# Layer 0's experts on token rows sorted by expert in DRAM, in tiles of 256 rows, instead of all experts on all tokens

## The reference

```python
x = _layernorm(x + _L0_attn_ref(x, ...))   # a linear recurrence over the sequence, then an MLP
x = _layernorm(x + _L0_ffn_ref(x, ...))    # top 2 of 8 experts
x = _layernorm(x + _L1_attn_ref(x, ...))   # attention, 16 heads of 8
x = _layernorm(x + _L1_ffn_ref(x, ...))    # top 2 of 4 experts, each expert an attention
```

```python
probs = softmax(input @ Wg)                       # 8 experts
top_vals, top_idx = top_k(probs, 2)               # shares: top_vals / their sum
xm = input[None] * moveaxis(mask, -1, 0)[..., None]
h = relu(einsum('ebsd,edh->ebsh', xm, W1) + b1)   # 128 -> 256
y = einsum('ebsh,ehd->ebsd', h, W2) + b2          # 256 -> 128
out = sum(y * moveaxis(scores, -1, 0)[..., None], axis=0)
```

## Time and profile before

| | us |
|---|---|
| median of 3 runs | 1557.26 (1551.56 to 1564.39) |
| the profiled execution, in all | 1544.68 |
| its span | 1542.9 |
| mean granted clock of TensorE, share of full | 0.911 |

### The profile page before, as it was taken

The page is one execution under the profiler, slowest core; times in us unless marked ns, Lnnn a source line. Parts: engine busy times, 40 slices in busy tenths (PEclk is TensorE's granted clock), DMA queues, the critical chain, the costliest instruction groups (busy, mean ns, idle before and its releaser), DMA issues.

```text
span 1542.9 us, 31463 instructions
## 1 busy us (share of the span) xinstructions
PE 1311.5 (85%) x12320; PEld 786.5 (51%) x12320; DVE 1017.0 (66%) x2422; ACT 767.9 (50%) x1260; POOL 525.6 (34%) x863
## 2 busy tenths in 40 slices
PE   4899999999655879889888899998989989988884
PEld 1566666667422335455445555555545545554543
DVE  3677667775444667777687777777777767757520
ACT  3334444433132356566465665665655656653540
POOL 1000010100342235346354454453544542442421
PEclk7999999999755879899899999999999999999986
DMA  7000000000000000101101011011010110110111
GB/s 206 1 1 1 1 1 1 0 1 1 0 1 9 9 2 9 38 11 33 31 13 42 18 26 37 8 42 31 13 42 5 39 36 9 42 36 10 32 34 36
DMA packets 34730, 35.03 MB, mean 23 GB/s; under 512 B 20070, under 2 KB 28440, under 8 KB 32536
## 3 DMA queue, kind: packets, MB, share of 16 engines
q1 hardware_dynamic: 34584, 33.03, 9.1%
HBM read 28.93 MB, written 2.88 MB: 21 GB/s over the span
## 4 chain that ended last, share of the span: by engine, by line
PE 44%; DVE 28%; SPq 7%; ACT 7%; POOL 5%; issue 5%; DMA 3%; DVEq 0%; ACTq 0%; POOLq 0%
PE ps L1367 17%; PE ps L634 14%; DVE mneg_e L1191 7%; PE ps L1445 7%; SPq L832 3%; PE ps L1468 3%; SPq L828 2%; DVE mneg_l L1191 2%; DVE acc L596 2%; DMA sums_l<-o_l 1%; SPq L850 1%; ACT probs L1038 1%; POOL q_low L915 1%; DMA sums_e<-o_e 1%; DVE equal L1217 1%
## 5 line engine op out<-in xcount | busy, mean ns | idle before, releaser
L1038 ACT ACTIVATE probs<-ps 128x1024 f32<-128x1024 f32 x384 | 389.8, 1024 | 244.9 <-PE ps L1367 243.9
L1191 DVE TENSOR_REDUCE mneg_e<-ps 128x2 f32<-128x512 f32 x512 | 337.1, 685 | 64.3 <-PE ps L1367 61.4
L1367 PE MATMUL ps<-k_high,q_high 32*128 32x256 f16 x1024 | 160.5, 283 | 50.6 <-DVE mneg_e L1191 41.3
L1191 DVE TENSOR_REDUCE mneg_l<-ps 128x2 f32<-128x512 f32 x256 | 167.8, 682 | 53.9 <-PE ps L1367 52.3
L1367 PE MATMUL ps<-q_high,k_high 32*128 32x256 f16 x1024 | 141.3, 276 | 4.1 <-ACT probs L1038 3.5
L1445 PE MATMUL ps<-probs,v_e 128*32 128x256 f32 x2048 | 138.6, 389 | 6.7 <-ACT v_e L1063 4.6
L1367 PE MATMUL ps<-q_low,k_high 32*128 32x256 f16 x1024 | 140.4, 273 | 0.0
L1367 PE MATMUL ps<-q_high,k_low 32*128 32x256 f16 x1024 | 139.6, 271 | 0.0
L428 ACT ACTIVATE h_moe<-ps,b 128x512 f32<-128x512 f32 x128 | 81.0, 684 | 116.9 <-PE ps L634 116.9
L634 PEld LDWEIGHTS ps<-w,h_moe 128*128 128x128 f32 x1024 | 122.1, 192 | 16.9 <-issue 16.7
L634 PE MATMUL ps<-w,h_moe 128*128 128x128 f32 x1024 | 124.6, 275 | 0.0
(11 more groups left out here) (216 smaller groups left out, 2393.6 us busy)
## 6 DMA issues: line engine op xcount, KB each, us to landing
on_e<-scratch_e SPq DMA_DIRECT2D x64, 256.0 KB, 4.6
on_l<-scratch_l SPq DMA_DIRECT2D x128, 32.0 KB, 1.9
sums_l<-o_l SPq DMA_DIRECT2D x128, 2.0 KB, 1.7
q_high<-shiftT_e SPq DMA_DIRECT2D x128, 2.0 KB
sums_e<-o_e SPq DMA_DIRECT2D x128, 4.0 KB, 1.7
out<-y SPq DMA_DIRECT2D x16, 128.0 KB, 2.0
w<-in_w SPq DMA_DIRECT2D x1, 1024.0 KB
qT<-shiftT_l SPq DMA_DIRECT2D x64, 2.0 KB
```

Source lines behind the costliest of these rows:

```text
L1038: act.activation(probs[:, probs_slot(r, i)].rearrange("p j s -> p (j s)"), s_banks(i).rearrange("p j s -> p (j s)"), ACT.Exp, scale=0.5 if ...
L1191: v.tensor_reduce(to, tiles(max_bank(k)), axis=AX, op=ALU.max, negate=True).then_inc(kind.max_used, 1)
L1367: return pe.matmul(o, l, r, start=start, stop=stop)
```

## The change

1. **Steps.** The 16 steps per chunk stay as the distance of two chunks, but each job gets a step of its own in a table `AT`, from -46 (`x_squares`) to 4 (the last scatters). A job with step s of chunk k is written at step s + 16 k. All of layer 0 up to the router is written this way, without expert products.
2. **Routing.** After the two experts are chosen, TensorE multiplies the 0/1 choice with a triangular and an all-ones matrix (`ranks`), which gives each token's rank among those of its expert. VectorE makes row numbers of it (`places`). GpSimd writes each tile of 128 tokens twice to DRAM, each row to its place (8 indirect DMAs per chunk). DRAM has one region for each expert, for each of two groups of 4 chunks; the regions are zeroed beforehand from SBUF (12 DMAs, 18.9 MB).
3. **Units.** When a group is complete, a table of tiles (256 rows of one expert each) is computed. A unit is two tiles; a group has 12 units (24 tiles, enough for any distribution). Per unit SyncE reads the table, loads two tiles of tokens (2 x 128 KB) and two experts' weights (2 x 329 KB) and stores two tiles of outputs over the tokens; TensorE transposes, multiplies to hidden and back; ScalarE copies and applies relu; VectorE adds b2.
4. **Sums.** GpSimd gathers each token's two outputs (8 indirect DMAs per chunk); VectorE adds them, times the shares, to x and normalizes.
5. **Order.** All layer 0 steps; the 12 units of group 0; the 12 units of group 1, between them the sums of group 0 (three pieces after each unit) and periods -6 to -4; then the periods from -3 on, with a piece of group 1's sums after every second slot.
6. **Smaller.** The gate is tanh, with its half in `wo0`, so there is no reciprocal; `mixer_scale` and `mlp_scale` are multiplied into weights once; GpSimd adds x and x1 (`xx`); scoreT and the b2 product are gone.

```diff
+STEPS = 16
+AT = {
+    "x_squares": -46, "x_rstd": -45, "xn": -43, "xT": -42, "xT_copy": -41, "kv_mm": -40, "k_copy": -39, "r_mm": -39,
...
+    "ranks": -4, "places": -3, "scatter": (-2, -1, 2, 4),
+}
...
-            for c in range(-2, CHUNKS + 1):
-                for i in range(STEPS if c < CHUNKS else LAST_STEPS):
-                    yield True, c, i
...
+            for u in range(FIRST_STEP, LAST_STEP + 1):
+                yield "layer0", u, None
+            for n in range(-1, UNITS + 1):
+                yield "experts", 0, n
+            prepared = [("attention", r, i) for r in range(FIRST_PERIOD, EARLY_PERIODS) for i in range(SLOTS)]
+            summed = list(sums_of(0))
+            done = 0
+            for n in range(-1, UNITS + 1):
+                yield "experts", 1, n
+                yield from summed[3 * (n + 1):3 * (n + 2)]
+                upto = len(prepared) * max(n, 0) // UNITS
+                yield from prepared[done:upto]
+                done = upto
...
+                    for t in range(CT):
+                        for k in due(u, AT["scatter"][t]):
...
+                            for n in range(2):
+                                pool.indirect_dma_start(by_expert[g], bass.IndirectOffsetOnAxis(ap=places[:, n, at:at + 1], axis=0),
+                                                        x_all[:, at, :], None).then_inc(z.scattered[g], DMA)
...
+                        if m == 0 and t == 0:
+                            for n in range(2):
+                                pool.wait_ge(ex.stored[n], DMA * PAIR * (UNITS // 2) * (g + 1))
...
+                    if 0 <= n < UNITS:
+                        q = UNITS * g + n
+                        act.wait_ge(ex.hidden_ps, q + 1)
...
+                                last = act.activation(h_moe[:, q % 2, k, at], hidden_bank[:, k, at], ACT.Relu, bias=b1)
...
+                        if t == 0:
+                            v.wait_ge(ex.gathered[k % 2], DMA * 2 * CT * (k // 2 + 1))
+                        token = k * CT + t
+                        for n in range(2):
+                            add = v.scalar_tensor_tensor(x_all[:, token, :], gathered[:, k % 2, n, t, :], shares[:, n, token:token + 1],
+                                                         x_all[:, token, :], ALU.mult, ALU.add)
+                            link(add)
```

## The result

The changed kernel takes 1569.46 us in the median of 11 runs (1559.95 to 1576.85); the kernel before, in turns with it, 1553.71 us (11 runs). The ratio is 1.0095 with a 95% interval of 1.0056 to 1.0133: slightly slower, at the very edge of the 1% bound. The forecast was 1581 us; the span forecast was 1566.8, the span of the profiled execution is 1565.2.

The account below looks back on a forecast made before the run. Layer 0 was taken as bound by TensorE, 224 of its 404 us being expert products. Forecast span: 437.5 to period -3, plus 24, plus 1105.3, 1566.8 us; 1581 us after scaling to the median; range 1500 to 1655.

Parts of the forecast that it names:

- The price p: GpSimd's time to issue one indirect DMA of 128 rows, for 64 scatters and 64 gathers; taken as 1.2 us.
- Rival 1: Faster through cheap issue: 0.43 us per indirect DMA, as on SyncE; 1518 us of span, 1532 as median; chance 0.32.
- rival 3: Slower through dear issue: VectorE's short SBUF operations delay scatters and gathers; at p = 2, 1658 us; chance 0.17.
- Rival 2: No change: p near 0.9, or the clock stays at 1.00 through the dense steps; about 1556 us; chance 0.18.
- Dense steps: Layer 0 ahead of the units: bound by hand-overs, 28.5 us per full chunk, ending at 247.5 us.
- 2 "of some 5" for the clock: Dense steps: half clock lengthens the cycle by some 5 us, 2 of them counted; pitch 28.5 instead of 26.5 us.
- Group 0's units: First twelve units: 5.6 us each, waiting for relu; 72 us in all, to 319.5.
- Rival 4: SyncE bounds the units: a table load near 1.5 us makes a unit 6.8 us; 29 more, 1610; chance 0.08.
- Group 1's units: Second twelve units: 34 us for the first two, 27 for the next four, 54 for the rest; sum 115 us.
- the remaining seven carry two prepared periods: End of group 1's units: 39 + 25 = 64 us one after the other, taken as 54, partly hidden in waits.
- The tail: From v_e's fill to the end: group 1's sums add 19 us in period -3 and 5 in period -2.
- All 224 us saved are spent: Layer 0's saved expert products go into longer dense steps and 187 us of units; v_e's fill stays near 437 us.

Follow-up runs that it names:

- e7: Changed kernel with GpSimd's sum xx 3 steps later (-26 in place of -29); 1563.71 us, ratio 1.0076 to the kernel before.
- e3: Changed kernel with the sums of group 0 begun two units later in group 1; 1580.18 us, ratio 1.0170 to the kernel before.

## Why the prediction was right, and where it was not

**The price p.** The choice of 1.2 us was the decisive one and right: 0.95 us busy, 1.26 from issue to issue. It was taken from another operation, a four-column power, and no run shows that the two have to do with each other: in that the number is luck. Rival 1 (0.43) and rival 3 (2 us) fall with it; rival 3's "from p about 1.1 it alone puts the time over 1% slower" was wrong, as p was 1.26 and the time 0.95% longer. Rival 2 had no change from p near 0.9 or from the clock staying at 1.00; the clock did not stay, and the issue's distance, which counts, is 1.26. By the Trainium skill (SBUF — State Buffer, "SBUF: two separate sides") a DMA issued by GpSimd that takes 0.62 us alone took 3.1 us beside a VectorE operation that holds the shared ports. Here the 64 scatters took 0.95 to 1.23 us to issue and 2.2 us in the median, 4.3 at most, from issue to landing beside VectorE's work, so the trace shows neither figure.

**Dense steps: 13 us short.** 247.5 was forecast for their end, the first scatter of the last chunk is at 260.7. The first chunk's is at 66.4 (64 forecast), and the pitch is 30.4, 30.4, 30.4, 30.7, 28.3 where the sum had 28.5. Step by step: x3 possible 7.7 us after the scatters' start, measured 7.7 (127.12 to 134.86, when x_all starts); the x root done at 11.4, measured 11.6; xn done at 12.3, measured 13.5. Here xn's price was wrong, 1.88 us for 0.87, because xx on GpSimd starts at the same moment. From xn to the next scatter 14.2 at full clock, and 2 "of some 5" for the clock, 16.2: measured 16.9. In e7, with the short xn and the clock at 0.83, xn to the next scatter took 13.6 us (109.68 to 123.29) and the whole pitch 26.2, the full-clock forecast being 26.5. So the chain was right and the two terms that failed are xn beside xx (1.0) and the clock (2.7 us over the forecast's 14.2, 3.3 over e7's 13.6, and not 2). The expectation that TensorE would be under 60% busy failed as well: 69%, since at the lower clock its work is longer.

**Group 0's units: right.** 72 us forecast, 69.7 measured (260 to 330), 5.5 us apart. TensorE in order of time, changed kernel:

```profile
282.70 0.63 PE L916 MATMUL ps<-ident,tokens 128*128 128x128 f32 x4 [1.42 <-DMA tokens<-by_expert]
...
288.60 2.02 PE L926 MATMUL ps<-expert_w,h_moe 128*128 128x128 f32 x16 [1.31 <-ACT h_moe L623]
...
294.10 2.02 PE L926 MATMUL ps<-expert_w,h_moe 128*128 128x128 f32 x16 [1.31 <-ACT h_moe L623]
```

They wait for relu, as forecast, and twice for tokens (1.42 and 1.53 us). Rival 4 (SyncE) did not occur.

**Group 1's units: 16 us too long.** VectorE in order of time:

```profile
346.42 1.51 DVE L813 SCALAR_TENSOR_TENSOR x_all<-gathered,shares,x_all 128x128 f32<-128x128 f32 x4 [16.31 <-DMA gathered<-by_expert,places]
348.24 0.75 DVE L788 TENSOR_TENSOR y_tokens<-ps,expert_w 128x256 f32<-128x256 f32 x2 [0.30 <-PE ps L926]
...
362.15 0.17 DVE L1613 TENSOR_TENSOR k_w<-qk_w 128x8 f32<-128x8 f32 x1 [4.92 <-POOL v_l L1217]
...
363.10 0.73 DVE L788 TENSOR_TENSOR y_tokens<-ps,expert_w 128x256 f32<-128x256 f32 x2
...
428.77 0.76 DVE L788 TENSOR_TENSOR y_tokens<-ps,expert_w 128x256 f32<-128x256 f32 x2 [3.87 <-PE ps L926]
```

The first two units: 34 us forecast, 33.7 measured, with both waits named, 16.31 us for gathers and 4.92 for GpSimd's fills. The next four: 27 forecast, 30.4 measured. The last term was mis-sized: "the remaining seven carry two prepared periods", 54 us. There are six, as 2 + 4 are gone of twelve, and they took 35.3 us: the preparation is nearly hidden in them. The group took 99.4 us and not 115.

**The tail: right in place and nearly in size.** +24 forecast, +27.9 measured from v_e to the end, of which 25.6 lie up to the fourth addition. Period -3: v_e to the first addition is 37.8 us, before 18.2; +19.6 where the sum had +19. Periods -2 and -1 have 3.8 and 3.2 more, where it had 5. The experiments support the cause (21 of 25.6 us are the sums, 16.6 of them the gathers) and refine it: beside the gathers VectorE's additions count for 1.6 us.

**The sum.** +13 in the dense steps, -2 in group 0's units, -16 in group 1's, +4 in the tail: 1565.2 of span against 1566.8. That is closer than the terms were; two errors of 13 and 16 us cancelled. The median lies 11.5 us under the forecast because the scale of 0.8% from one execution to the median was too large: from this profiled execution (1567.02 in all) it was 0.16%, and the kernel before, timed again, had 1553.71 instead of 1557.26. "All 224 us saved are spent" was nearly right: 5.6 of them are left at v_e. Slower by over 1% was given 0.47 and within 1% 0.20; the time ended at 0.95%, in the less likely class, though not by rival 2's mechanism.

## What to carry to other kernels

Work that is cut from the bounding engine is worth only what the next chain lets through. Here the price of the new work was 1.26 us of GpSimd per 128 gathered or scattered rows, 128 times, and it counted only where it stood in front of something waited for, so the same operations are 4.5% apart by order alone (1569 and 1499 us). Before stages are put one behind the other (steps, then units), look whether one has idle time on the engine that bounds the other. And moving a wait away from one operation (e3) helps only if what is put off doesn't meet other work later.

## What the runs showed of the hardware

GpSimd's and VectorE's operations on SBUF can exclude each other. xn (four operations of 128x128) takes 0.87 us alone and 1.88 beside xx (1.25 us). The first of the four takes 1.29 us and ends 0.08 us behind xx (140.04 against 139.96 in the chunk above), and the other three are as short as ever, some 0.2 us each: it isn't a shared rate, it is a wait for xx. One such first operation by itself, in the changed kernel, with xx at 169.43:

```profile
169.47 1.29 DVE L682 TENSOR_SCALAR xn<-x_all,rstd 128x128 f32<-128x128 f32 x1 [2.67 <-POOL rstd L464]
```

By the Trainium skill (SBUF — State Buffer, "SBUF: two separate sides") the pair of ports that GpSimd and VectorE share is an exclusive lock: of a GpSimd operation and a VectorE operation that uses it, the one that starts first keeps it for its whole instruction. By that rule xn would be longer by what is left of xx, 1.21 us; the trace has 1.01, so it agrees but for 0.2 us. That xn is such an operation no row says. The wait can be longer than one operation: once, at 23.70, the first of the four took 3.42 us, until 27.12, and beside it GpSimd had xx and, right behind it, a run of small fills that ended at 27.04. xn of x1 (L720, 0.87 us), which starts 0.05 us ahead of one of GpSimd's four-column roots, isn't longer; there GpSimd's own two operations are 0.29 and 1.12 us instead of 0.19 and 1.04.

In dense steps whose work and order hardly differ, TensorE's clock can be at either level for some 8 us of a chunk: six records took 4.48 us in the changed kernel and 2.82 in e7, after a wait of 1.75 or 0.75 us that came behind two others of 3.2 to 3.4 and 1.3 us. In that chunk the clock was worth three times the wait itself (26.2 us instead of 30.4; 1.0 of these 4.2 us is xn's). What decides it the runs don't settle: e7 has three of its five chunks at the lower level with the wait as short, and the changed kernel one at the higher with the wait as long.
